# Another instruction order on all five engines of a cross-attention and quantised feed-forward kernel, and SwiGLU written as (t+1)(g u)

## The reference

```python
x = x + xattn(layernorm(x), ctx, ctx, Wq, Wk, Wv, Wo)   # 32 heads of 32, 8 key/value heads
x = x + ffn(layernorm(x))
# ffn, on bfloat16 rows:
qg, sg = quant(x * inv_gate);  qu, su = quant(x * inv_up)      # per row: scale = max|.|/127, round
gate = (qg @ w_gate.T) * sg * s_wgate
up   = (qu @ w_up.T)   * su * s_wup
inter = clip(silu(gate) * up, -10, 10).astype(bfloat16)
qi, si = quant(inter * inv_inter)
out  = (qi @ w_down.T) * si * s_wdown
```

## Time and profile before

| | before |
|---|---|
| median of 3 runs | 764.09 us (756.08 to 766.71) |
| profiled execution, its own time | 766.03 us |
| its span in the trace | 764.2 us |
| PE busy | 686.0 us, 90% |
| DVE, ACT, POOL busy | 475.5, 285.9, 260.8 us |
| mean granted clock of PE | 0.969 of full |
| DMA traffic | 93.71 MB, mean 123 GB/s |

### The profile page before, as it was taken

The page is one execution under the profiler, slowest core; times in us unless marked ns, Lnnn a source line. Parts: engine busy times, 40 slices in busy tenths (PEclk is TensorE's granted clock), DMA queues, the critical chain, the costliest instruction groups (busy, mean ns, idle before and its releaser), DMA issues.

```text
span 764.2 us, 14196 instructions
## 1 busy us (share of the span) xinstructions
PE 686.0 (90%) x5840; PEld 449.4 (59%) x5840; DVE 475.5 (62%) x772; ACT 285.9 (37%) x449; POOL 260.8 (34%) x207
## 2 busy tenths in 40 slices
PE   3999999989899989999899979999899988997853
PEld 3989888867466646654556646664556543443321
DVE  4562514633566856786747665877647566967863
ACT  4443042373515242435133425253433334343221
POOL 3363130120315134334241534241543235355431
PEclk9999999999999999999989999999999989999967
DMA  9695633769442171235222363233312343211100
GB/s 344 207 364 169 215 98 109 222 216 298 118 167 57 36 223 34 81 94 166 63 80 69 80 177 80 50 101 119 101 47 80 122 118 79 97 57 62 53 27 27
DMA packets 45191, 93.71 MB, mean 123 GB/s; under 512 B 5176, under 2 KB 21560, under 8 KB 45112
## 3 DMA queue, kind: packets, MB, share of 16 engines
q1 hardware_dynamic: 42824, 84.43, 36.0%
q0 software_dynamic: 2304, 8.39, 2.8%
HBM read 70.65 MB, written 22.15 MB: 121 GB/s over the span
## 4 chain that ended last, share of the span: by engine, by line
PE 60%; DMA 21%; SPq 5%; DVE 4%; ACT 4%; POOL 3%; issue 2%; POOLq 0%; ACTq 0%
PE bank L788 14%; PE bank L701 14%; PE bank L814 6%; DMA wv_lo<-r_dram 5%; PE bank L663 4%; PE bank L676 4%; DMA k_stack<-k_dram 4%; DMA max_dram<-max_rows 3%; PE bank_s L720 3%; PE bank L836 3%; PE bank_o L752 3%; PE bank_s L738 3%; PE bank_d L757 3%; DMA r_dram<-r_sb 2%; PE bank L802 1%
## 5 line engine op out<-in xcount | busy, mean ns | idle before, releaser
L701 PE MATMUL bank<-act_t_hi,wq_hi 128*128 128x256 f16 x512 | 140.4, 274 | 0.0
L701 PE MATMUL bank<-act_t_lo,wq_hi 128*128 128x256 f16 x512 | 140.2, 274 | 0.0
L701 PE MATMUL bank<-act_t_hi,wq_lo 128*128 128x256 f16 x512 | 140.1, 274 | 0.0
L2191 DVE TENSOR_REDUCE neg_max<-bank_s 128x4 f16<-128x512 f32 x128 | 84.7, 684 | 54.2 <-PE bank_s L720 53.7
L1622 ACT ACTIVATE probs<-bank_s 128x512 f32<-128x512 f32 x128 | 73.0, 598 | 88.3 <-PE bank_s L738 66.7
L2808 POOL TENSOR_TENSOR wv_hi<-wv_hi,wv_lo 128x512 f32<-128x512 f32 x28 | 37.2, 1334 | 114.5 <-DMA wv_lo<-r_dram 108.2
L1658 ACT COPY q_t<-bank 128x1024 f16<-128x1024 f16 (+1 forms) x48 | 41.8, 871 | 74.3 <-PE bank L802 61.9
L2802 POOL TENSOR_TENSOR xs<-xb,inv_gate 128x1024 f32<-128x1024 bf16 x16 | 35.4, 2211 | 88.0 <-DVE xb L2221 88.0
L738 PE MATMUL bank_s<-q_stack,k_stack 97*128 97x512 f16 x128 | 45.1, 387 | 13.7 <-DMA q_stack<-max_dram 9.1
L701 PEld LDWEIGHTS bank<-act_t_hi,wq_hi 128*128 128x128 f16 x512 | 50.3, 98 | 10.3 <-issue 1.1
L701 PEld LDWEIGHTS bank<-act_t_lo,wq_hi 128*128 128x128 f16 x512 | 50.4, 98 | 9.6 <-issue 0.3
(11 more groups left out here) (145 smaller groups left out, 1372.1 us busy)
## 6 DMA issues: line engine op xcount, KB each, us to landing
q_stack<-q_dram SPq DMA_DIRECT2D x48, 256.0 KB, 4.4
inp<-in_x SPq DMA_DIRECT2D x16, 512.0 KB, 6.0
wv_lo<-r_dram SPq DMA_DIRECT2D x14, 512.0 KB
x<-in_x SPq DMA_DIRECT2D x11, 512.0 KB, 4.2
out<-x POOLq DMA_DIRECT2D x11, 512.0 KB, 3.0
q_dram<-q_st_hi SPq DMA_DIRECT2D x8, 512.0 KB, 4.0
q_dram<-q_st_lo SPq DMA_DIRECT2D x8, 512.0 KB, 5.1
w_gate<-in_ctx_t SPq DMA_DIRECT2D x6, 512.0 KB, 6.4
```

Of the source, the lines that this page charges most:

```text
L701: ins = nc.tensor.matmul(bank[:, :, jj, :], wq_sb[a][:, 2 * item + jj, kc, :], act_t[m][:, kc, :, :], start=(kc == 0 and (a, m) == PARTS[0 ...
L2191: nc.vector.tensor_reduce(neg_max[:, c:c + REP], bank_s[g % 2][:, :].rearrange("p (j n) -> p j n", j=REP), AX_X, ALU.max, negate=True).the ...
```

## The change

It has four parts.

1. The call lists of all five engines are written in another order. The calls are the same, except that `wo_` is cut at other places (740 calls on PE's list instead of 737; the matmuls are the same) and that DVE's list has 17 more (below).
2. `swiglu` is split. `swg` multiplies g and u (`tensor_tensor`), as soon as both are there, and `swiglu` then makes (t+1) times the product. The factor 0.5 is left out, the clip goes to ±20, and the rows `inv_inter` are halved once by `half_rows`.
3. `half_rows` stands on DVE's list between `v(6, 0)` and `v(6, 1)`, and waits for the six row loads of `load_rows`; these stand on SP's list behind `spill_v(5)` and `spill_k(5)`.
4. `pv(r, 0)` waits for the reciprocals of block r-1, instead of those of block r-2.

```diff
-                if t == 0 and needed(r - 1):
-                    pe.wait_ge(recip_done, r - 1)
+                if t == 0 and needed(r):
+                    pe.wait_ge(recip_done, r)
...
+            def swg(p, b):
+                r = 2 * p + b
+                dve.wait_ge(gu_scaled, 2 * r + 2)
+                nc.vector.tensor_tensor(u_buf[:, :], g_buf[:, :], u_buf[:, :], ALU.mult).then_inc(swiglu_step, 1)
+
             def swiglu(p, b):
 
                 r = 2 * p + b
+                dve.wait_ge(swiglu_step, 2 * r + 1)
                 dve.wait_ge(tanh_done, r + 1)
-                nc.vector.scalar_tensor_tensor(g_buf[:, :], t_buf[:, :], 1.0, g_buf[:, :],
+                nc.vector.scalar_tensor_tensor(u_buf[:, :], t_buf[:, :], 1.0, u_buf[:, :],
                                                ALU.add, ALU.mult).then_inc(swiglu_step, 1)
-                dve.wait_ge(swiglu_step, 2 * r + 1)
-                dve.wait_ge(gu_scaled, 2 * r + 2)
-                nc.vector.scalar_tensor_tensor(u_buf[:, :], g_buf[:, :], 0.5, u_buf[:, :],
-                                               ALU.mult, ALU.mult).then_inc(swiglu_step, 1)
                 dve.wait_ge(swiglu_step, 2 * r + 2)
...
-                nc.vector.tensor_scalar(inter[:, :], u_buf[:, :], LIMIT, -LIMIT, ALU.min, ALU.max).then_inc(inter_ready, 1)
+                nc.vector.tensor_scalar(inter[:, :], u_buf[:, :], 2 * LIMIT, -2 * LIMIT, ALU.min, ALU.max).then_inc(inter_ready, 1)
+
+            def half_rows():
+                dve.wait_ge(rows_loaded, 16 * 6)
+                nc.vector.tensor_scalar(invi_sb[:, :], invi_sb[:, :], 0.5, None, ALU.mult).then_inc(rows_halved, 1)
 
             def quant_i(p, b):
                 r = 2 * p + b
                 dve.wait_ge(inter_ready, r + 1)
+                dve.wait_ge(rows_halved, 1)
```

More of the change, by code:

```diff
@@ L526, in _ @@
             fill_q(2, 0)
+            fill_v(2, 0)
             save_r(1, 1)
@@ L580, in _ @@
             load_res(3, 1)
+            fill_v(4, 1)
+            load_x(7, 1)
+            spill_q(5)
             fill_q(5, 0)
             fill_k(5, 0)
+            fill_v(5, 0)
+            save_r(4, 1)
+            load_x(7, 0)
+            fill_r(4, 1)
             save_max(5, 0)
-            save_r(4, 1)
-            fill_v(5, 0)
             fill_max(5, 0)
-            fill_r(4, 1)
             load_res(4, 0)
@@ L590, in _ @@
             fill_k(5, 1)
+            save_r(5, 0)
             load_res(4, 1)
+            fill_r(5, 0)
             save_max(5, 1)
+            fill_v(5, 1)
+            fill_max(5, 1)
             spill_q(6)
[L594 to L597, removed]
             fill_q(6, 0)
             fill_k(6, 0)
+            save_max(6, 0)
+            load_res(5, 0)
+            fill_max(6, 0)
             save_r(5, 1)
@@ L618, in _ @@
             save_r(6, 1)
+            fill_r(6, 1)
             save_max(7, 0)
@@ L1199, in _ @@
-            mt(3, 1)
-            wo_(2, 1, 0, 7, 8)
+            pv(3, 0, 1)
+            gu(1, 1, "up")
+            wo_(2, 1, 0, 0, 6)
+            s(3, 1, 0)
+            wo_(2, 1, 0, 6, 7)
+            s(3, 1, 1)
+            wo_(2, 1, 0, 7, 8)
+            wo_(2, 1, 1, 0, 1)
+            s(3, 1, 2)
+            s(3, 1, 3)
+            wo_(2, 1, 1, 1, 3)
+            s(3, 1, 4)
+            s(3, 1, 5)
+            xt(5, 1, 1)
+            wo_(2, 1, 1, 3, 4)
+            s(3, 1, 6)
+            wo_(2, 1, 1, 4, 5)
@@ new lines, in _ @@
+            mt(5, 0)
+            wo_(4, 0, 0, 5, 7)
+            q(6, 1, 3)
+            wo_(4, 0, 0, 7, 8)
+            wo_(4, 0, 1, 0, 3)
+            st(5, 0, 0)
+            wo_(4, 0, 1, 3, 4)
+            st(5, 0, 1)
+            st(5, 0, 2)
+            q(6, 2, 0)
+            st(5, 0, 3)
+            wo_(4, 0, 1, 4, 5)
+            st(5, 0, 4)
+            pv(5, 0, 0)
+            wo_(4, 0, 1, 5, 6)
+            st(5, 0, 5)
+            st(5, 0, 6)
+            wo_(4, 0, 1, 6, 8)
+            ti(3, 0)
@@ L2598, in _ @@
             max_(5, 0, 1)
+            ln2_stats(3, 1)
+            ln2_apply(3, 1)
             max_(5, 0, 2)
-            lo(6, "q1")
-            ln2_apply(3, 1)
+            gscale(3, 0, 1)
             max_(5, 0, 3)
+            recip(4, 1)
             max_(5, 0, 4)
@@ L2712, in _ @@
             quant(5, 1, 1)
+            ln2_stats(6, 0)
+            ln2_apply(6, 0)
+            gscale(5, 1, 0)
             recip(7, 0)
+            quant(6, 0, 0)
             max_(7, 1, 0)
             max_(7, 1, 1)
+            gscale(5, 1, 1)
             max_(7, 1, 2)
@@ L2928, in _ @@
             xs_(3, 0, 1)
[L2929 removed]
+            norm(4, 0, 1)
             o_lo(4, 0, 0)
[L2931 to L2932 removed]
             fin(2, 1)
+            rstd2_(3, 1)
             o_lo(4, 0, 1)
[L2935 removed]
             xs_(3, 1, 0)
@@ L2987, in _ @@
             fin(6, 0)
+            rstd2_(7, 0)
             norm(7, 1, 1)
```

1600 lines of the change are left out of this document (785 added, 815 removed).

## The result

The changed kernel takes 776.75 us (median of 4 runs, 771.67 to 778.79), the kernel before 763.6 us beside it: a ratio of 1.0169, with a 95% interval of 1.0090 to 1.0248. It is slower, by about 1.7%. The forecast was 750 us, with 736 to 769 as its range. The profiled execution has a span of 773.8 us, 9.6 more than before.

A forecast was written before the change was run, and what follows sets the result against it. PE's own work was taken to bound the long middle, a chain through all engines the last 74 us. The terms sum to -14.2 us: 766.0 to 751.8 us profiled, 750 us as median, range 736 to 769.

The forecast's parts named there:

- k_stack: PE's waits for k_stack in the middle: more PE work covers the fill, 7.2 us falls to 1.5, so -5.7 us.
- v_cur: PE's one wait for v_cur: its fill now stands ahead of save_r and fill_r, so the wait goes, -4.8 us.
- The codes: PE's wait for one block's codes: code_i(5, 0) now stands ahead of a late o_hi on ACT, -2.7 us.
- exp: PE's waits for exp, 4.1 us in the middle: no place named as mended, 0 us, bounds -4 and +4.
- The maxima: Maxima's trip through memory: shorter cover, reciprocals' fill ahead of the save in more blocks, +3 us, bounds -9.1 and +15.
- the slower rival: The 8 KB write caught behind the reciprocals' fill in many blocks: 783 us for seven; above 770 us, chance 0.10.
- The clock: Four low-clock windows of PE lie at stalls that go; of their 9.1 us 8 are taken, -8 us.
- The start and half_rows: DVE may be a few us late with v(6, 1) for the row loads, mostly hidden by PE's work, +1 us.
- SwiGLU and the wait of pv: Two multiplications before and after; pv's wait for the previous block's reciprocals has 6.9 us of distance: 0 us each.
- The tail: Last wo_ starts 2 us later, then 1.3 us more on DVE before the last two blocks: +3 us, bounds -3.4, +6.
- the rule cited in the prediction: Each DMA engine consumes one queue's descriptors in ring order, so a small write behind SP's large read waits for it.

The follow-up runs named there:

- Experiment 5: The changed kernel with the tail order of before on ACT, DVE and POOL, and ACT's hi(4,q0) behind mt_copy(2,1): 770.31 us, ratio 1.0007 to the kernel before.
- experiment 3: The kernel before with everything of the change except the new order (split SwiGLU, halved rows, wait of pv): 767.84 us, ratio 1.0005.
- Experiments 2: The changed kernel with its tail on ACT, DVE and POOL in the order of before, except one pair of POOL calls: 776.91 us, ratio 1.0118 to the kernel before.
- experiment 4: The changed kernel with save_max and fill_max of all blocks issued by ACT behind mt_copy instead of by SP: 791.37 us, ratio 1.0312 to the kernel before.

## Why the prediction was wrong, step by step

- **k_stack**, -5.7 us forecast: 7.2 to 2.6, so -4.6. Nearly right.
- **v_cur**, -4.8: the wait at 378 us went, one of 2.6 us came at 572; -2.2. I looked only at the place of the old wait.
- **The codes**, -2.7: right.
- **exp**, 0: the waits of 4.1 us went, which no place in the lists had let me name.
- **The maxima**, +3: this step failed. The mechanism stands there as it is, with blocks 10, 11 and 14 as the places, but the term is +15. I sized it as three writes at a small price. Seven were caught, because I looked for late pv's ("most blocks stay clear of the fill") and not for the distance of the two issues on SP's list: in six of the seven save_max leaves d = 2.7 to 6.1 us behind fill_r, and the write lands 8.2 to 11.5 us behind fill_r, 9.8 in the mean. So it takes about 9.8 - d us, and PE waits for what is above some 3. The 8.86 us in flight of the earlier trace rows would have given nearly this for every block. A list of PE's work can't show it; what holds the write up are the four DMA engines that the read runs on. The price for one was near what I gave the slower rival (5 us); over the seven it was 2.7 us each, as the read has a head start.
- **Block 5**, in no step: 4.9 us of the 15, from an instruction of another stage that stands ahead of mt_copy on ACT and waits for a spill. Experiment 5 freed the copy; half of the wait then came from the read in flight.
- **The clock**, -8: it followed the stalls. PE is busy 2.0 us longer for the same work of the middle. Three of the four dips of the earlier trace rows are gone. The one at 620 us is still there and deeper (0.71, where it was 0.77), behind a wait of 1.2 us for k_stack, and new ones stand at new stalls, at 150, 190, 310, 490, 530 and 570 us. Two windows of PE of the changed kernel:

```profile
150.00:160.00 10.00, 7.71 (x48) 0.67 0.63 215
490.00:500.00 10.00, 10.00 (x78) 0.78 0.01 3
```

  The sum gave away its largest term for stalls it had not yet ruled out elsewhere.
- **The start and half_rows**, +1: DVE waited 1.6 us for the rows, and PE did not wait behind it. A new wait of 2.7 us for q_st_lo at 196 us has another source: DVE stood at an x load in flight for 12.95 us, issued behind the reciprocals' reads and a piece of the weights.
- **SwiGLU and the wait of pv**, 0: experiment 3 has it at 1.0005.
- **The tail**, +3: 5.9, beyond the work moved. The last wo_ was to start 2 us later; it starts 5.3 us later behind the last pv, of which 3.7 are work moved, so 1.6: right, with rstd2_, the copy and the gu as named. The second part, forecast at 1.3 us, was mis-sized: 4.0 us. ln2_stats ahead of dn held up the codes, and quant(7, 1, 0) ahead of gscale(7, 0, 1) put the second product of block 14's SwiGLU beside POOL's xs (below). Experiments 2 and 5 gave it back.

In sum: the idle time of the middle was forecast at -9 us and came out at +1.6; the clock at -8, and it came out at +2.0; the tail at +3, and it was 5.9. The result lies inside the rival "slower", which had one chance in ten: its mechanism is the one that the runs show, and its blocks are seven. What speaks against it in the prediction was read from PE's list alone.

What stays open: by the granted clock of the windows of 10 us the middle lost 17.1 us at full clock instead of 12.0, so 5 more; its busy time says 2.0. A part of the gap is low clock in idle time, which costs nothing: over PE's busy time alone the loss is 14.9 us instead of 11.0, which is still 3.9 against 2.0. Why the waits for exp of before went isn't traced to a move. And no run spreads the reciprocals' read over more than four DMA engines, which would test the four engines directly and might shorten the read itself.

## What to carry to other kernels

When small round trips share the DMA engines with large reads, list for each trip the distance between its issue and that of the last large read, in both orders, and see how many DMA engines the large one runs on: here 8 KB behind a read of 512 KB on four engines waits for the rest of that read, while the other twelve engines are free. A stall that an order removes is only gain if the same list is gone through for every other trip: here 13.5 us of removed waits gave 8 us, and 19 us of them gave nothing as long as the late read had an o_hi and an exp behind it on another engine. In this tail, which is one chain, calls moved ahead of the one that the chain waits for cost their time and their waits too, and putting them back gave both back.

## What the runs showed of the hardware

**A write behind a large read, on two queues.** The reciprocals' read runs on four of the sixteen DMA engines (a DMA share of 0.25 in the window of block 10, and four late steps of its semaphore, as the section on the result reads them), and a write of 8 KB that has parts on all sixteen is done only when those four are. From SP's queue the maxima land 8.2 to 11.5 us after the issue of the read (the six blocks above), 9.8 in the mean; from ACT's queue 7.8 to 10.9 us after it, 9.4 in the mean (blocks 3, 8, 9, 10, 11 and 14 of experiment 4, 1.7 to 5.9 us between the issues). On one queue each of the last four parts lands 0.17 to 0.21 us behind the read's, so the rule cited in the prediction, ring order within one queue, fits there; it can't be the whole cause, since the write from the second queue is late too. The Trainium skill (DMA: Bandwidth & Descriptors, Queues, rings and completion order) says that a DMA engine takes turns between its queues, packet by packet. From that one would expect a write from the second queue to land early, and the measurement says that its last parts came 0.7 to 1.7 us ahead of the read's in blocks 10, 11 and 14, and not ahead of them in blocks 8 and 15: the queue made little difference.

**DVE beside GpSimd.** The second product of SwiGLU, 128x512 with two inputs, takes 0.70 us alone. Of its sixteen executions in the changed kernel the six that begin while POOL's xs_ runs take 1.65 to 2.56 us and end 0.5 us behind it; the other ten take 0.63 to 0.69. In the tail, where POOL's xs_ runs from 737.88 to 740.01 us, it took 2.55:

```profile
738.00 2.55 DVE L2267 SCALAR_TENSOR_TENSOR u_buf<-t_buf,u_buf 128x512 f32<-128x512 f32 x1
```

```profile
737.88 2.13 POOL L2830 TENSOR_TENSOR xs<-xb,inv_up 128x1024 f32<-128x1024 bf16 x1 [3.72 <-ACT code_g L1683]
```

The Trainium skill (GPSIMD Engine Reference, Specifications) has it that GpSimd shares its SBUF interfaces with VectorE and contends with instructions of two SBUF inputs; the trace agrees.
